# Attention, a long convolution and a routed expert layer in one kernel: probabilities of 22 of 32 head pairs turned by transposing DMAs instead of on TensorE

## The reference

```python
x = x + attention(layernorm(x))            # 16 heads, d_head 128, rotary, causal softmax, biases
x = x + gated_convolution(layernorm(x), k, skip, ctx)   # y = causal conv of v*ctx with filter k, + kv*skip, then sum with ctx
x = x + experts(layernorm(x))              # 16 experts, top 4 of softmax(x @ gate), plus one shared expert with a sigmoid gate
```

## Time and profile before

| | |
|---|---|
| median of 3 runs | 954.27 us (952.92 to 955.51) |
| the profiled execution, its own time | 953.62 us |
| its span, first to last instruction | 951.8 us |
| PE busy | 911.5 us, 96% |
| DVE busy | 778.2 us, 82% |
| POOL, ACT busy | 503.2 us, 438.8 us |
| mean granted clock | 0.993 |

### The profile page before, as it was taken

One profiled execution on the slowest core, in us unless ns is written; L12 is line 12 of the kernel. 1 busy time (PEld: TensorE's weight loads), 2 busy tenths in 40 slices (PEclk: granted clock), 3 DMA queues, 4 the chain that ended last, 5 costly groups with the idle time before them and its releaser, 6 DMA issues.

```text
span 951.8 us, 19467 instructions
## 1 busy us (share of the span) xinstructions
PE 911.5 (96%) x6305; PEld 818.4 (86%) x6305; DVE 778.2 (82%) x1704; ACT 438.8 (46%) x1227; POOL 503.2 (53%) x380
## 2 busy tenths in 40 slices
PE   7899999999999999999999999989998799999996
PEld 6798888989899888998888888877887699999985
DVE  6988877977887999877799877767779688888867
ACT  3656655454334663333564333462156244444431
POOL 1433424465453436776354677525617377777760
PEclk9999999999999999999999999999999899999999
DMA  7796399899157952303793221315151277777768
GB/s 270 252 364 227 131 320 389 313 395 362 46 182 250 401 208 89 112 25 123 292 370 113 91 110 55 120 62 237 60 209 69 69 130 127 131 130 127 134 115 311
DMA packets 75584, 179.08 MB, mean 188 GB/s; under 512 B 7776, under 2 KB 42464, under 8 KB 74464
## 3 DMA queue, kind: packets, MB, share of 16 engines
q1 hardware_dynamic: 61040, 158.80, 46.0%
q0 software_dynamic: 14448, 19.05, 12.1%
HBM read 98.35 MB, written 79.47 MB: 187 GB/s over the span
## 4 chain that ended last, share of the span: by engine, by line
PE 80%; DVE 7%; issue 5%; POOL 3%; ACT 2%; DMA 1%; SPq 0%; DVEq 0%; ACTq 0%
PE bank L550 11%; PE bank L552 10%; PE bank L551 10%; PE bank L854 6%; PE bank L632 6%; PE bank L956 4%; POOL xs L1352 3%; PE bank L832 3%; PE bank L834 3%; PE bank L836 3%; PE bank L618 3%; PE bank L658 3%; PE bank L660 3%; PE bank L659 3%; PE bank L914 2%
## 5 line engine op out<-in xcount | busy, mean ns | idle before, releaser
L1312 POOL TENSOR_TENSOR z_lo<-prob_t,z_hi 128x512 fp32r<-128x512 f32 x64 | 82.5, 1297 | 188.5 <-ACT z_hi L1199 169.4
L1516 DVE SCALAR_TENSOR_TENSOR turn<-bank,bqk,trig 128x1024 f32<-128x1024 f32 x128 | 160.6, 1276 | 23.3 <-PE bank L552 20.8
L1344 POOL TENSOR_TENSOR rot<-turn 128x512 f32<-128x512 f32 x64 | 96.0, 1500 | 110.0 <-DVE turn L1516 94.6
L1405 POOL DMA_INDIRECT sums<-ysb,token_at x79 | 123.3, 1561 | 56.6 <-DMA sums<-ysb,token_at 28.0
L550 PE MATMUL bank<-xt_hi,w_hi 128*128 128x512 f32 x256 | 105.7, 413 | 3.4 <-DVE xt_lo L1480 1.7
L1185 ACT COPY prob_t<-bank 128x512 f32<-128x512 f32 x64 | 37.5, 586 | 148.8 <-PE bank L618 142.1
L1144 ACT ACTIVATE prob<-prob,negmax 128x128 f32<-128x128 f32 x256 | 99.1, 389 | 2.5 <-DVE negmax L1501 2.4
L552 PE MATMUL bank<-xt_hi,w_lo 128*128 128x512 f32 x256 | 100.1, 391 | 0.0
L551 PE MATMUL bank<-xt_lo,w_hi 128*128 128x512 f32 x256 | 99.7, 390 | 0.0
L1352 POOL DMA_INDIRECT xs<-xh,dest x64 | 74.3, 1161 | 41.2 <-issue 37.4
L1155 ACT COPY v<-bank 128x512 f32<-128x512 f32 x64 | 37.6, 587 | 114.5 <-PE bank L552 113.5
(11 more groups left out here) (197 smaller groups left out, 2643.3 us busy)
## 6 DMA issues: line engine op xcount, KB each, us to landing
xs<-zeros SPq DMA_DIRECT2D x16, 2120.0 KB, 15.3
w_hi<-w_dram SPq DMA_DIRECT2D x24, 768.0 KB, 9.7
w_lo<-w_dram SPq DMA_DIRECT2D x24, 768.0 KB, 9.1
xe_all<-xs SPq DMA_DIRECT2D x79, 132.5 KB
wo_hi<-wo_dram SPq DMA_DIRECT2D x26, 256.0 KB, 9.1
wo_lo<-wo_dram SPq DMA_DIRECT2D x26, 256.0 KB, 10.1
sums<-zeros SPq DMA_DIRECT2D x3, 2176.0 KB, 12.8
raw<-in_wqkv SPq DMA_DIRECT2D x16, 384.0 KB, 4.5
```

What stands on the lines that cost most here:

```text
L1344: nc.gpsimd.tensor_tensor(rot[m][1][:], turn[m][1], turn[m][2], ALU.add).then_inc(rot_pool, 1)
L1405: nc.gpsimd.indirect_dma_start(sums_dram[s % SUMS], bass.IndirectOffsetOnAxis(ap=token_at[:, s:s + 1], axis=0), ysb[s % YBUFS][:], None, c ...
L1516: last = nc.vector.scalar_tensor_tensor(turn_all[m][:, 2 * i:2 * i + 2, :], qk_bank[2 * m + i][:].unsqueeze(1).to_broadcast([128, 2, GT]), ...
```

## The change

For the 22 pairs t = 8 to 29 (`by_dma`), which are weighed in steps s = t + 2, that is (1, 2) to (3, 7), the transposes on PE and their two copies out of the bank are gone. Instead:

- ACT splits each head's probabilities into their two 16-bit halves (`prob_planes`, 128 x 1024 values of 16 bits): head 0 of the pair as ACT's last work of step s-1, head 1 in step s behind the copies of V;
- SP stores the 256 KB to memory (`prob_store`), waits until they have landed, and loads them back with a transposing DMA (`prob_turn`) into `prob_t`; head 0, then head 1, and behind both the step's weight loads and fills;
- PE's `weigh_values` of head 0 comes behind QE (at p = 0 and p = 3 ahead of it), that of head 1 behind KE;
- the second half of V is no longer put between the weighings, `cross_back` and `token_turn` come ahead of the scores, `token_logits` ahead of QE;
- on DVE head 1's probabilities are normalised ahead of `rot`; on POOL head 0's ahead of the first rotation, and `z_low` of head 1 between the rotations; on ACT exponentials and z's high part alternate by head;
- FILL_STEPS: two parts each at (1, 0), (1, 1), (1, 4), (1, 5), (1, 6), one each at (1, 2), (1, 3), (1, 7), (2, 1), (2, 2), (2, 3), none in group 3; the `sums` are zeroed in group 3 instead of group 2.

A few semaphores are merged into others with higher counts; no instruction goes with them.

```diff
+FILL_STEPS = ([(1, p) for p in (0, 0, 1, 1)] + [(1, p) for p in (2, 3, 4, 4)] + [(1, p) for p in (5, 5, 6, 6)]
+              + [(1, 7)] + [(2, p) for p in (1, 2, 3)])
+def by_dma(t):
+    return PAIRS <= t < PAIRS * GROUPS - 2
...
+            def prob_store(t, h):
+                sp.wait_ge(planes_ready, 2 * dma_before(t) + h + 1)
+                rows = prob_dram[t % 2, h].rearrange("(b q i) k -> q b i k", b=GB, i=2)
+                sp.dma_start(rows, planes[h][:]).then_inc(prob_stored, 16)
+
+            def prob_turn(t, h):
+                sp.wait_ge(prob_stored, 16 * (2 * dma_before(t) + h + 1))
+                sp.wait_ge(z_lo_done, 2 * (t - 1) + h + 1)
+                sp.dma_start_transpose(prob_t[h][:].rearrange("p b q -> p (b q)").unsqueeze(1).bitcast(U16),
+                                       prob_dram[t % 2, h]).then_inc(prob_landed[h], 16)
...
+                    t = g * PAIRS + p - 2
+                    if by_dma(t):
+                        prob_store(t, 0)
+                        prob_turn(t, 0)
+                        prob_store(t, 1)
+                        prob_turn(t, 1)
+                    if 0 < p < PAIRS - 1:
+                        load_w(g, p + 1)
+                        load_o(g, p + 1)
...
             def weigh_values(s, p, h, first):
-                pe.wait_ge(pt_taken, s * 2 - 4 + h + 1)
+                t = s - 2
+                if by_dma(t):
+                    pe.wait_ge(prob_landed[h], 16 * (dma_before(t) + 1))
...
+                by_pe = live(2) and not by_dma(s - 2)
+                if by_pe:
                     transpose_probs(s, 0, live, order)
...
+                elif live(2):
+                    between_weighings(g, p, live)
+                    if p in (0, 3):
+                        weigh_values(s, p, 0, first)
+                    if p == 2 and g > 1:
+                        pe.wait_ge(v_taken, s * 2)
+                        token_logits(g - 2, pt_bank)
                 beside_second(g, p, live)
                 for i, col in enumerate((QE, QO, KE, KO)):
...
+                    if live(2) and not by_pe and i == 0 and p not in (0, 3):
+                        weigh_values(s, p, 0, first)
+                    if live(2) and not by_pe and i == 2:
+                        weigh_values(s, p, 1, first)
...
+            def prob_planes(t, h):
+                act.wait_ge(prob_ready[h], t + 1)
+                if dma_before(t):
+                    act.wait_ge(prob_stored, 16 * (2 * dma_before(t) + h - 1))
+                nc.scalar.copy(planes[h][:], prob[h][:].bitcast(U16).rearrange("p b (k i) -> p b i k", i=2)).then_inc(planes_ready, 1)
...
-                        if h == 1 and live(2):
-                            dve.wait_ge(pt_ready, s * 2 - 2)
+                        if by_dma(s - 2):
+                            dve.wait_ge(planes_ready, 2 * dma_before(s - 2) + h + 1)
...
+                if by_dma(s - 1):
+                    second_probs()
```

More of the change, by code:

```diff
@@ L188, in decoder @@
         zeros = sb("zeros", [128, 4, XW], c=tctx)
+        planes = [sb(f"planes{h}", [128, GB, 2, SEQ], U16, tctx) for h in range(2)]
         tctx.close()
@@ L297, in decoder @@
         prob_ready = [sem(f"prob_ready{h}") for h in range(2)]
+        planes_ready = sem("planes_ready")
+        prob_stored = sem("prob_stored")
+        prob_landed = [sem(f"prob_landed{h}") for h in range(2)]
         pt_ready = sem("pt_ready")
@@ L385, in value_order @@
         def value_order(g, p, live):
-            late = live(1) and live(2) and (p in (1, 2) or (g == 0 and p > 2))
+            late = live(1) and live(2) and (p in (1, 2) or (g == 0 and p > 2)) and not by_dma(g * PAIRS + p - 2)
             return (1, 0) if late else (0, 1)
@@ L785, in project_values @@
                     q = (p - 1) % PAIRS
-                    if half == 0 and p == 2 and g > 1 and live(0):
-                        pe.wait_ge(tl_done, CH * (g - 1))
                     pe.wait_ge(qk_used, s * 4 - 2 + half)
@@ L815, in step @@
                     token_turn(2)
+                h = g - 1
+                if p == 2 and 1 < g < GROUPS:
+                    two_banks_free(g, p, live)
+                    pe.wait_ge(v_taken, s * 2 - 1)
+                    token_turn(h - 1)
                 if live(3):
@@ L1023, in _ @@
             pe.wait_ge(slot_ready, 1)
-            nc.tensor.transpose(banks[1][0:2, 256:384], slot[:], ident[:]).then_inc(slot_turned, 1)
+            nc.tensor.transpose(banks[1][0:2, 256:384], slot[:], ident[:])
             pe.wait_ge(diag_ready, 1)
```

203 lines of the change are left out of this document (119 added, 84 removed).

## The result

The changed kernel takes 992.67 us (median of 4 runs, 989.71 to 994.28), beside 954.89 for the kernel before on the same chip (952.92 to 957.95): ratio 1.0385, 95% interval 1.0356 to 1.0413. The forecast was 949.5, faster. It is 38 us slower.

The account below looks back on a forecast made before the run. PE was taken as the bound (busy 911.5 of 951.8 us), DVE close behind; 22.7 - 11.6 - 4.1 - 0.5 + 1.8 - 3.5 = 4.8 us off 953.6 gives 948.8, 949.5 after adjusting to the runs' median. Range 940 to 967.

Parts of the forecast that it names:

- The transfers: Stores and turns of the probabilities: 3.5 us lost, 1.5 in (1, 2) and 2 in (1, 3), otherwise hidden.
- the queue is mostly empty: SP's queue in groups 2 and 3, given as the argument against a late round trip of the probabilities.
- The first stores: Head 0's first store, behind group 1's fills and weights: turn lands at 175, wanted at 173.2; 1.5 us of wait.
- The 10.5 us a head: Eight transposed squares at the skill page's 1309 ns each, an alternative turn time against the 3.0 us taken.
- a round of SP of 22.3 us: Steps (1, 4) to (1, 6): 18.8 us of transfers plus about 3.5 us of empty queue, against 21.2 us steps.
- The first rival: Late round trip of the probabilities, deciding at head 1 in steps without filters: slower by 16 us, 965; chance 0.28.
- What is removed: Both heads' transposes on PE: 1.03 us a step, 22.7 us in 22 steps.
- the steps with filters: Twelve steps, p >= 4: PE waits 0.97 us for DVE before f+3, 11.6 us come back; step 21.2 us.
- The three waits for ACT: Three weighings waiting 0.55, 0.69 and 0.54 us for ACT to empty the bank: waits go, 1.8 us gained.
- Pairs (2, 2) and (2, 3): DVE-bound, like (3, 2) and (3, 3): no gain taken, so 4.1 us come back over both pairs.
- ACT's copy: Copy of 1024 16-bit halves on ACT: about 1.07 us by elements or 0.59 by bytes, hidden.
- The sum without transfers: All terms over the 22 steps except the 3.5 us for transfers: 22.7 - 11.6 - 4.1 - 0.5 + 1.8.

Follow-up runs that it names:

- free kernel: Changed kernel without stores and turns, ACT copying the probabilities straight into the turn's tile, so nothing is transposed: 950.6 us, 0.9972 of the kernel before.
- first experiment: Changed kernel with only the zero fills moved: spread over groups 1 to 3, sums tables all zeroed in (3, 7): 972.6 us, 1.0185 of the kernel before.
- e11: e10 plus head 0's weighing ahead of filter f+3 and POOL's scatter wait moved ahead of the next four scatters: 953.5 us, 0.9981 of the kernel before.
- e14b: e11 with the round trip from (2, 0) on, fills two each in (1, 0) to (1, 6), one in (2, 4), (2, 5): 942.6 us, 0.9915.
- e10: Changed kernel with the round trip only from (2, 2) on, all fills in group 1, sums in (0, 6), (0, 7): 955.8 us, 1.0023.
- e6: Changed kernel, fills spread, sums in (2, 4) to (2, 6), head 0's weighing ahead of filter f+3 in steps with filters: 972.3 us, 1.0207.

## Why the prediction was wrong, step by step

**The transfers: this step failed.** I wrote 3.5 us lost, "PE waiting for DMA only in (1, 2) and (1, 3)", and that "in groups 2 and 3 the queue is mostly empty". It cost 44. Each transfer alone was sized well: in an empty queue a store was followed by its turn after 2.3 to 2.6 us (I took 2.8), and PE started 3.1 us after the turn's issue (3.0). The first stores, in (1, 2), cost 1.4 us of waiting (1.5); (1, 3) cost 5.6 (2). By the Trainium skill's 261 GB/s ("DMA: Bandwidth & Descriptors", Latency and other measured facts), a figure for turns whose middle dimension is not contiguous, the turn would be about 3 us, an estimate: the 3.1 us agree. The 10.5 us a head worked out from the Trainium skill's page "VectorE: DVE Perf Modes" (The three transpose paths) did not appear. What I did not do is to write down what the engines still hold at the moment when each store is issued, and to carry it on. For two fills I had a round of SP of 22.3 us against steps of 21.2, and took the excess as covered by the filters' 6 us. It took 26.9 to 28.5 us: stores and turns held the engines some 5.2 us a step and not the 2.6 of their bytes at 398 GB/s, and the engines stood free for about 5 us a round and not 3.5. So each such step left about 6 us to the next and not 1.1, and the gap from store to turn grew from 11.39 in (1, 5) to 17.16 us in (1, 6). For one fill in a step of 17 us I had no sum at all. "Mostly empty" was false at exactly the steps where the change's own list puts fills and sums: (2, 1) to (2, 3), (3, 1) to (3, 3). By my own figures weights and fill start 8 us behind the start of V, 5.1 us into (2, 2) as steps are counted here, need 10.7, and the next store comes at 15.5: no room, but hardly a wait. That shows the danger and not its size. In the trace the gap from store to turn goes 2.32, 5.94, 11.33 us over (2, 1), (2, 2), (2, 3), and weights and fill start only at 9.9 us. The first rival had the cause, transfers standing behind others, but not the place: it looked for the lateness at head 1, in ten steps without filters, and all six long waits are head 0's, two of them in steps with filters, while head 1's turn followed its store after 2.5 to 2.6 us in all of them. It was given 0.28 and 965, because its upper bound was the one row of a store behind others, 6.6 us; the stores here took up to 17.

**The clock: not foreseen.** In (1, 3), (1, 6), (1, 7) and (2, 0) 8.4 us stand beyond the waits, and the half speed behind them accounts for 8.1; in (2, 3) and (3, 3) it is there too, 4.5 us, against waits of the free kernel that are gone. The rows of before had no such idle time in the loop, and its granted clock there was 1.00.

**What is removed, and the steps with filters: right.** 176 transposes are gone. f+3 waits for DVE; here in (2, 5):

```profile
428.59 0.59 PE L710 MATMUL bank<-kv,toep 128*128 128x256 f32 x2
429.81 0.70 PE L708 MATMUL bank<-kv,toep 128*128 128x256 f32 x2 [0.63 <-DVE zc L1676]
```

The row gives 0.63 us of idle time; by starts, as the 0.97 was reckoned, f+3 comes 1.22 us behind the last product of f+2 instead of 0.43, 0.79 us late. I said 21.2 us for the step; (1, 4) is 21.29 and (3, 7) 21.29. The three waits for ACT that were to go did: with free turns (2, 7), (3, 6) and (3, 7) are 0.75, 0.84 and 0.74 us shorter than before. (2, 5) and (3, 5) are 22.63 and 22.32: POOL reaches z's low part late. The first experiment's trace shows it standing in the wait for four scatters while the DMA engines are at a share of 0.94 to 1.05:

```profile
396.56 0.96 POOL L1446 DMA_INDIRECT xs<-xh,dest  x1 [0.30 <-issue]
403.07 1.29 POOL L1397 TENSOR_TENSOR z_lo<-prob_t,z_hi 128x512 fp32r<-128x512 f32 x1 [5.54 <-DMA xs<-xh,dest]
```

ACT had finished z's high part at 401.14. Before, in (2, 5), the same wait ended 1.74 us after the last scatter; in (3, 0), where the engines' share was 0.98 to 1.06, it took 5.82 there too. With the wait moved and the weighing ahead of f+3 (e11, e14b) these steps are 20.9 us; e10, without both, has 22.8. With the weighing alone, in e6, (2, 5) is 20.89 and (3, 5) 23.72 us, so what the scatter wait is worth by itself was not cleanly measured.

**Pairs (2, 2) and (2, 3): right as a sum, wrong in its parts.** I took no gain, and (2, 2) "no more than a few tenths shorter". With free turns (2, 2) is 17.09 instead of 20.13 and (2, 3) 21.66 instead of 18.87: 38.75 against 39.00. DVE's work had not got less, it fell due one step later. In (3, 2) and (3, 3) the sum did fall, 37.16 against 38.99.

**ACT's copy: right.** 1.04 to 1.05 us for 1024 elements of 16 bits (1.07 by elements), hidden.

**The sum without transfers.** 4.8 + 3.5 = 8.3 us; the free kernel's steps gave 4.6 us and its median 0.28% (0.04 to 0.52%). The sign was right, the size too high: the twelve steps with filters gave 1.5 us (I had 12 x 1.03 - 11.6 + 1.8 = 2.6), the ten others 3.1 (I had 5.7). Step (1, 1), which I had not looked at, is 1.2 us longer in every kernel with the new order from (1, 2) on, the free one included; its cause is open.

## What to carry to other kernels

Before a short transfer is put on a critical path, list for each step what the DMA engines still hold when it is issued, in us, add the times in which the queue stands empty waiting for a landing, and carry what is left over into the next step; its own latency in an empty queue says little. Another issuing engine does not take it past the bulk, so the bulk has to be moved to other steps or the round trip kept out of crowded ones. A freed engine pays only where the next wait behind it is also filled, as with the weighing in the place of filter f+3's wait.

## What the runs showed of the hardware

- A store of 256 KB and the turning load of it took about 2.6 us of all 16 DMA engines together (an estimate from the queue's shares before and after), 200 GB/s, beside some 400 GB/s for weights and fills; SP was held 1.16 us by most turning loads, 2.24 us at most.
- A store issued beside a fill on another queue took as long to its turn as behind it on the same one (11.42 and 11.33 us); with neither ahead it was 2.32.
- SP was held up to 12.01 us in issuing one load when two large fills and the weights were outstanding.
- In six waits of 3.6 to 6.6 us PE's granted clock went to the 1.2 GHz level, and PE then ran 3.0 to 6.0 us of work at it.
- POOL's wait for four scatters ended 1.74 us after the last one in a quiet stretch and 5.54 and 5.82 us after it (first experiment, kernel before) where the DMA engines' share was about 1.0.
